# Gated delta rule on one core: the keys of the state scaled on ScalarE, the triangle multiplied in two passes, and TensorE's work put in another order

## The chip, the core and the metric

One core of a Trainium2 chip runs one launch of the whole program. The metric is the device time of that launch in microseconds (us), median of three runs. The engines are TensorE (PE in the rows, its weight loads PEld), VectorE (DVE), ScalarE (ACT), GpSimd (POOL) and SyncE (SP), which issues the DMAs.

## The reference, cut to what matters

The program is four stages on 8 sequences of 512 rows of 256 numbers: attention, a gated FFN with FP4 weights, the gated delta rule, and an FFN with ternary weights. Only the third is touched. Of it:

```
q = l2norm(q) * dk ** -0.5;  k = l2norm(k)            # per head, dk = dv = 128, 8 heads
g = cumsum(g) within chunks of 64 rows
decay = tril(exp(g[i] - g[j]))
tri = tril((k_beta @ k.T) * decay, -1)                # 64 x 64 in each chunk
Tm = inverse(eye + tri)
v_new = Tm @ v_beta;  k_cum = Tm @ (k_beta * exp(g))
for each chunk:                                       # 8 chunks of a sequence, in order
    attn = tril(q @ k.T * decay)
    v_n = v_new - k_cum @ S
    out = (q * exp(g)) @ S + attn @ v_n
    S = S * exp(g_last) + (k * exp(g_last - g)).T @ v_n
```

## The kernel before, in words

**Tiling and staging.** `delta_rule` works on pairs of heads: 8 sequences x 4 pairs are 32 pairs, `e` is the head within a pair. All matmuls are float32; each is issued as two passes, so `x4` in a row of the trace is two matmuls. The loop `for q in range(-1, PAIRS)` runs the scan of pair `q` beside the front of pair `f = q + 1`, and every engine has its own copy of that loop, in program order; semaphores alone tie them together. An iteration has three parts. In the first, `n` goes from 0 to 8: the scan of pair `q` does chunk `m = n`, and the functions `front_early`, `front_middle` and `front_late` lay pieces of the front of pair `f` between its steps (projections `keys_in`, `gate_in`, `values_in`, `queries_in`; the convolution as taps on VectorE; transposes `keys_across`; the products `key_gram`; the norms `key_norms`). In the second, `l` goes from 1 to 5: the levels of the block inverse of pair `f`. At each level TensorE multiplies `NT` by `L` (L2025, "z"), ScalarE copies that to `ZS` (L1516), TensorE multiplies by `U` (L2042 and L2047, "y"), and VectorE puts the result into `U` and `L` (L1605, L1607). The third part makes the attention rows, the new values and the cumulated keys (L2068, L2076).

**A step of the scan.** TensorE multiplies `PQ` by the state `S` (L1981, "p1"); VectorE makes the new values `V2` from it (L1757, "w"), ScalarE copies the query half to `O` (L1503); TensorE multiplies `V2` by the keys `KK` (L1999, "ds"), and VectorE updates `S` (L1773). In odd chunks TensorE multiplies `AT` (L2012, "oi"), and VectorE updates `O` (L1785). The first chunk has no state: its ds takes 64 rows of `VV` and `KK` in place of the 128 rows of `V2` and `KK` that the others take, of which one half is zero.

**What the change touches.** `keys_to_state` (L1561) scales the transposed keys in the PSUM bank `F0` into `KK`, `keys_to_inverse` (L1565) into `KE`, both on VectorE; `values_in` then overwrites `F0`. `lower` (L1592) makes the triangle `NT` = `F1` x `cneg` x `gb`, four instructions for each head, where `cneg` are the norm factors that `key_scales` makes on GpSimd (it ends at L1346) out of the sums of `key_norms` (L1569, L1571), and `gb` the decays. `lower_across` (L1911) transposes `NT`, `first_level` (L1599, L1601) fills `U` and `L` and frees `F1` for `queries_in`. After the last pair of a sequence come the output projection and the residual; in the next pair `statistics` (L1640, L1643) and `normalize` (L1648) run on VectorE at steps 4 and 8.

## Time and profile before

| | us |
|---|---|
| median of 3 runs (lowest, highest) | 3079.18 (3071.64, 3082.57) |
| the profiled execution, its own time | 3079.22 |
| its span | 3077.5 |
| PE busy | 2880.1 (94%) |
| DVE busy | 2246.7 (73%) |
| ACT busy | 1231.3 (40%) |
| POOL busy | 1018.6 (33%) |
| the loop over pairs with scan and front, 1061 to 2806: length | 1745.00 |
| PE, DVE, ACT, POOL busy in it | 1715.55, 1354.44, 742.80, 443.46 |

A row of the timeline has the start, the busy time (of xcount instructions in one run), the engine, the line of the kernel, the operation, the tiles written and read, and in brackets the idle time before it and what ended it. Matmuls are pipelined, and their busy times overlap. How long a run holds TensorE is therefore the distance from its start to the start of the next row, not its busy time.

### The profile page before, as it was taken

What the parts mean: (1) busy time and instruction counts of PE and PEld (TensorE: products, weight loads), DVE (VectorE), ACT (ScalarE), POOL (GpSimd) and SP (SyncE); (2) the same over time, 40 slices, a digit from 0 to 9 for tenths busy, and PEclk for the clock granted to TensorE, in tenths of its full rate; (3) what the DMA queues carried; (4) which work ended last, traced back from release to release, by engine and by line L of the source; (5) the groups of instructions that cost most, each with busy time, mean ns of one, the idle gap of its engine ahead of it and who ended that gap; (6) DMA issues with size and microseconds to landing.
All of it is one profiled execution on the core that took longest, in us unless ns stands there. A gap on an engine that the chain in (4) does not pass through costs nothing. (4 is left out here: it accounts for less than half of the span.)

```text
span 3077.5 us, 81016 instructions
## 1 busy us (share of the span) xinstructions
PE 2880.1 (94%) x32507; PEld 2008.8 (65%) x32507; DVE 2246.7 (73%) x5235; ACT 1231.3 (40%) x2975; POOL 1018.6 (33%) x1495
## 2 busy tenths in 40 slices
PE   6999999849997899999999999999999999998897
PEld 3444444336664677777787777777777777776565
DVE  4666677778885687687788778678678678685566
ACT  1433333413333344344444345345344344342454
POOL 2554555526883222223223222222122222231011
PEclk8999999969998899999999999999999999999899
DMA  2121111100001111010010010100100001000000
GB/s 86 34 52 40 30 31 30 28 7 1 1 1 30 31 47 36 19 33 23 19 36 20 23 33 19 33 23 19 33 23 29 23 23 33 19 19 2 9 21 28
DMA packets 85332, 80.36 MB, mean 26 GB/s; under 512 B 54480, under 2 KB 67808, under 8 KB 84960
## 3 DMA queue, kind: packets, MB, share of 16 engines
q1 hardware_dynamic: 84960, 75.18, 8.7%
q8 instruction: 260, 4.26, 0.6%
q14 instruction: 112, 0.92, 0.1%
HBM read 57.70 MB, written 4.85 MB: 20 GB/s over the span
## 5 line engine op out<-in xcount | busy, mean ns | idle before, releaser
L1842 PE MATMUL gd_bk<-gd_xT,gd_wh 128*128 128x512 f32 x768 | 394.3, 623 | 1.8 <-DVE gd_xT L1742 0.9
L480 DVE TENSOR_REDUCE at_nm<-at_ring 128x2 f32<-128x256 f32 (+3 forms) x256 | 199.1, 820 | 143.1 <-PE at_ring L623 143.1
L1547 DVE SCALAR_TENSOR_TENSOR gd_YK<-gd_bk,gd_cw,gd_YK 128x511 f32<-128x511 f32 (+2 forms) x384 | 283.1, 743 | 10.3 <-ACT gd_YK L1413 4.7
L1516 ACT COPY gd_ZS<-gd_bk 128x256 f32<-128x256 f32 x320 | 119.1, 372 | 299.0 <-PE gd_bk L2025 292.7
L2025 PE MATMUL gd_bk<-gd_L,gd_NT 64*64 64x64 f32 x5120 | 203.3, 222 | 14.4 <-DVE gd_L L1607 7.3
L1605 DVE COPY_PREDICATED gd_U<-gd_mU,gd_bk 128x128 f32<-128x128 int32 x320 | 103.8, 326 | 146.7 <-PE gd_bk L2047 112.2
L2025 PEld LDWEIGHTS gd_bk<-gd_L,gd_NT 64*64 64x64 f32 x5120 | 170.1, 134 | 61.3 <-issue 33.6
L2042 PE MATMUL gd_bk<-gd_U,gd_ZS 64*64 64x64 f32 x5120 | 207.6, 221 | 0.1
L2042 PEld LDWEIGHTS gd_bk<-gd_U,gd_ZS 64*64 64x64 f32 x5120 | 174.7, 135 | 40.9 <-issue 37.1
L302 POOL TENSOR_TENSOR at_PT<-at_PT,at_dm 128x1024 f32<-128x1024 f32 (+3 forms) x128 | 197.8, 1545 | 10.7
L561 PE MATMUL at_ring<-at_QT,at_KT 32*128 32x512 f32 (+3 forms) x1024 | 168.6, 504 | 17.5 <-DVE at_PT L452 12.7
L1842 PEld LDWEIGHTS gd_bk<-gd_xT,gd_wh 128*128 128x128 f32 x768 | 127.5, 192 | 86.2 <-issue 72.1
L1503 ACT COPY gd_O<-gd_bk 64x128 f32<-64x128 f32 x448 | 105.7, 259 | 194.1 <-PE gd_bk L1981 191.9
L1999 PEld LDWEIGHTS gd_bk<-gd_V,gd_KK 128*128 128x128 f32 x896 | 125.4, 190 | 74.1 <-DVE gd_V L1757 54.0
L1999 PE MATMUL gd_bk<-gd_V,gd_KK 128*128 128x128 f32 x896 | 151.3, 291 | 15.7 <-DVE gd_V L1757 13.3
L1981 PEld LDWEIGHTS gd_bk<-gd_S,gd_PQ 128*128 128x128 f32 x896 | 129.9, 192 | 52.3 <-issue 39.1
L1757 DVE SCALAR_TENSOR_TENSOR gd_V<-gd_bk,gd_cneg,gd_VV 64x128 f32<-64x128 f32 x448 | 138.3, 347 | 33.5 <-PE gd_bk L1981 30.1
L1323 POOL TENSOR_TENSOR gd_zz<-gd_zz,gd_nw_row 128x512 f32<-128x512 f32 x64 | 80.2, 1274 | 248.1 <-ACT gd_zz L1435 248.1
L2047 PE MATMUL gd_bk<-gd_ZS,gd_U 64*64 64x64 f32 x4096 | 162.0, 218 | 0.0
L336 ACT ACTIVATE at_PT<-at_ring 128x1024 f32<-128x1024 f32 (+3 forms) x128 | 90.1, 704 | 178.8 <-PE at_ring L561 178.8
L299 POOL TENSOR_SCALAR_AFFINE_SELECT at_PT<-at_PT 128x256 f32<-128x256 f32 x128 | 54.1, 423 | 296.0 <-ACT at_PT L336 295.3
L338 ACT ACTIVATE at_PT<-at_PT 128x1024 f32<-128x1024 f32 (+3 forms) x128 | 94.3, 737 | 138.9 <-DVE at_PT L452 138.7
(355 smaller groups left out, 6755.5 us busy)
## 6 DMA issues: line engine op xcount, KB each, us to landing
...
gd_gb<-gates SPq DMA_DIRECT2D x128, 64.0 KB, 3.3
...
at_QT<-at_QS SPq DMA_DIRECT2D x128, 32.0 KB, 2.0
at_KT<-at_KS SPq DMA_DIRECT2D x128, 32.0 KB, 2.0
at_OC<-at_Ob SPq DMA_DIRECT2D x128, 32.0 KB, 2.0
at_RC<-inverse SPq DMA_DIRECT2D x128, 32.0 KB, 1.8
...
```

The source lines that it names most:

```text
L302: nc.gpsimd.tensor_tensor(PT[s % RP][:, 2:GH, 0:n], PT[s % RP][:, 2:GH, 0:n], dm[:, 0:n].unsqueeze(1).broadcast_to([P, 2, n]), ALU.mult).t ...
L480: nc.vector.tensor_reduce(nm[v % 2][:, k, c0:c0 + HS + 1:HS], set_of(s, 2 + p)[:, :, 0:n], AX.X, ALU.max).then_inc(max_done, 1)
L561: last_ = nc.tensor.matmul(set_of(s, p)[:, i, 0:n], KT[lane(u)][r, k * P:(k + 1) * P], QT[lane(u)][r, k * P:W], start=True, stop=True)
L1516: nc.scalar.copy(ZS[e][:, :, :], chunks(A_[e])).then_inc(zs_done[e], 1)
L1547: nc.vector.scalar_tensor_tensor(out[:, s:W], bank_[:, 0:W - s], cw[:, j, head(f, e), CONVK - 1 - s:CONVK - s], out[:, s:W], ALU.mult, ALU ...
L1757: nc.vector.scalar_tensor_tensor(V2[e][rows(c), t % 2, c, :], A_[e][rows(c), 0:DK], cneg[q % 2][rows(c), e, t:t + 1], VV[e][rows(c), t, :] ...
L1842: ins = nc.tensor.matmul(out[:, :], wh[:, k, e, col * DK:(col + 1) * DK], xT[:, k, :], start=k == 0, stop=k == DC - 1)
L1981: nc.tensor.matmul(A_[e][:, 0:DK], PQ[e][q % 2][:, m // CPT, m % CPT, :, :].rearrange("p s n -> p (s n)"), S[e][:, :], start=True, stop=Tr ...
L1999: nc.tensor.matmul(A_[e][:, DK:2 * DK], fixed, moving, start=True, stop=True).then_inc(ds_mm[e], 1)
L2025: last = nc.tensor.matmul(A_[e][rows(c), t * CK:(t + 1) * CK], NTm[e][rows(c), t, :], L[e][rows(c), t, :], start=True, stop=True)
L2042: last = nc.tensor.matmul(A_[e][rows(c), (TPS + t) * CK:(TPS + t + 1) * CK], ZS[e][rows(c), t, :], U[e][rows(c), t, :], start=True, stop=True)
L2047: last = nc.tensor.matmul(A_[e][rows(c), t * CK:(t + 1) * CK], U[e][rows(c), t, :], ZS[e][rows(c), t, :], start=True, stop=True)
```

## The change

It does this, all in the delta rule:

- `keys_to_state` goes from VectorE (one 128x512 instruction a head) to ScalarE (four 128x128), at n = 3 and 4; `keys_to_inverse` comes on VectorE to n = 3 and 4, both `key_norms` to the end of n = 4.
- `lower` becomes one VectorE instruction a head (`F1` x `gb`), without the wait for the norm factors; GpSimd multiplies `NT` by `cneg` behind `key_scales`.
- The first chunk's ds takes 128 rows like the others; ScalarE copies 64 rows of `VV` into `V2` for it.
- On TensorE both `lower_across` stand together at n = 7, all `queries_in` at n = 8, both `values_across` together at level 3, and the last `values_in` of head 1 is cut into two halves around the ds of step 6.
- Taps are spread otherwise over the levels, `queries_out(f, 0)` goes from level 3 to 5 on ScalarE, `statistics` to the start of a pair, `normalize` to the first step of the pair after.

```diff
@@ gpsimd, key_scales
                     nc.gpsimd.tensor_scalar(cneg[f % 2][:, :, :], cc[:, :, :], -1.0, 0.0, ALU.mult, ALU.add).then_inc(rk_done, 1)
+                    pool.wait_ge(rk_done, f + 1)
+                    for e in E2:
+                        pool.wait_ge(ng_done, f * 2 + e + 1)
+                        nc.gpsimd.tensor_tensor(NTm[e][:, :, :], NTm[e][:, :, :], cols(cneg[f % 2][:, e, :])[:, :, 0:CK], ALU.mult).then_inc(nt_done[e], 1)
@@ scalar
+                def keys_to_state(f, e):
+                    act.wait_ge(kk_done[e], f + 1)
+                    for t in range(TPS):
+                        last = nc.scalar.activation(KK[e][f % 2][:, t, :], F0[e][:, t * P:(t + 1) * P], ACT.Copy, scale=column(KF_, f, e, t))
+                    last.then_inc(ks_done[e], 1)
...
                         gate_out(f, 1)
+                        keys_to_state(f, 0)
+                    if n == 4:
+                        keys_to_state(f, 1)
...
-                        if l == 3 and has(f):
-                            queries_out(f, 0)
                         if l == 4 and has(q):
                             heads_out(q, 0)
                             heads_out(q, 1)
                         if l == 5 and has(f):
+                            queries_out(f, 0)
                             queries_out(f, 1)
...
                             for c in range(CPT):
-                                last = nc.scalar.copy(PQ[e][f % 2][:, :, c, c, :], chunks((A_[e], F1[e])[c]))
-                            last.then_inc(kc_done[e], 1)
+                                nc.scalar.copy(PQ[e][f % 2][:, :, c, c, :], chunks((A_[e], F1[e])[c]))
+                        for e in E2:
+                            act.wait_ge(vnc_done[e], f + 1)
+                            nc.scalar.copy(V2[e][rows(0), 0, 0, :], VV[e][rows(0), 0, :]).then_inc(kc_done[e], 1)
@@ vector, lower
-                    dve.wait_ge(rk_done, f + 1)
                     dve.wait_ge(e_done[e], f + 1)
                     dve.wait_ge(gk_mm[e], f + 1)
                     ge(dve, z_mm[e], f * (LEVELS - 1))
-                    for t in range(TPS):
-                        last = nc.vector.scalar_tensor_tensor(NTm[e][:, t, :], F1[e][:, t * CK:(t + 1) * CK], cneg[f % 2][:, e, t:t + 1],
-                                                              gb[e][f % 2][:, t, :], ALU.mult, ALU.mult)
-                    last.then_inc(nt_done[e], 1)
+                    nc.vector.tensor_tensor(NTm[e][:, :, :], chunks(F1[e]), gb[e][f % 2][:, :, :], ALU.mult).then_inc(ng_done, 1)
@@ vector, the loop
+                        if n == 0 and ends_seq(q - 1):
+                            statistics(seq(q - 1))
...
-                        if n == 4 and ends_seq(q - 1):
-                            statistics(seq(q - 1))
-                        if n == 8 and ends_seq(q - 1):
-                            normalize(seq(q - 1))
+                        if n == 0 and ends_seq(q - 2):
+                            normalize(seq(q - 2))
@@ tensor
                 def values_in(f, e, k):
-                    pe.wait_ge(kk_done[e], f + 1)
+                    pe.wait_ge(ks_done[e], f + 1)
                     project(F0[e], e, 2, k, vp_mm[e])
+
+                def values_half(f, e, half):
+
+                    cut = slice(half * W // 2, (half + 1) * W // 2)
+                    ins = nc.tensor.matmul(F0[e][:, cut], wh[:, DC - 1, e, 2 * DK:3 * DK], xT[:, DC - 1, cut], start=False, stop=half == 1)
+                    if half == 1:
+                        ins.then_inc(vp_mm[e], 1)
...
                                 if m == 0:
-                                    pe.wait_ge(vnc_done[e], q + 1)
                                     pe.wait_ge(kc_done[e], q + 1)
-                                    fixed, moving = KK[e][q % 2][rows(c), t, :], VV[e][rows(c), t, :]
```

Three places of the program as the engines get it, each within one ordinary pair. First TensorE at the start of a pair, before and then of the change (L1842 and L1845 are `keys_in`, L1999 and L2007 ds, L1981 and L1994 p1):

```order
L2076 MATMUL gd_bk<-gd_U,gd_KE 128x64 x16
L1842 MATMUL gd_bk<-gd_xT,gd_wh 128x512 x2
L1999 MATMUL gd_bk<-gd_VV,gd_KK 128x128 x2
L1842 MATMUL gd_bk<-gd_xT,gd_wh 128x512 x2
L1981 MATMUL gd_bk<-gd_S,gd_PQ 128x128 x2
```

```order
L2080 MATMUL gd_bk<-gd_U,gd_KE 128x64 x16
L1845 MATMUL gd_bk<-gd_xT,gd_wh 128x512 x2
L2007 MATMUL gd_bk<-gd_V,gd_KK 128x128 x2
L1845 MATMUL gd_bk<-gd_xT,gd_wh 128x512 x2
L1994 MATMUL gd_bk<-gd_S,gd_PQ 128x128 x2
```

The order is the same; the ds between the two projections now reads `V2`, 128 rows of it. Second, TensorE from p1 of step 6 to the second level, before and of the change (L1911 and L1920 are `lower_across`, L2012 and L2019 oi, L2025 and L2032 z, L1878 the halves):

```order
L1981 MATMUL gd_bk<-gd_S,gd_PQ 128x128 x2
L1842 MATMUL gd_bk<-gd_xT,gd_wh 128x512
L1999 MATMUL gd_bk<-gd_V,gd_KK 128x128 x2
L1911 MATMUL gd_bk<-gd_identc,gd_NT 64x64 x8
L1981 MATMUL gd_bk<-gd_S,gd_PQ 128x128 x2
L1911 MATMUL gd_bk<-gd_identc,gd_NT 64x64 x8
L1999 MATMUL gd_bk<-gd_V,gd_KK 128x128 x2
L2012 MATMUL gd_bk<-gd_V,gd_AT 64x128 x4
L1842 MATMUL gd_bk<-gd_xT,gd_wh 128x512 x2
L2025 MATMUL gd_bk<-gd_L,gd_NT 64x64 x16
L1842 MATMUL gd_bk<-gd_xT,gd_wh 128x512 x2
L2042 MATMUL gd_bk<-gd_U,gd_ZS 64x64 x8
```

```order
L1994 MATMUL gd_bk<-gd_S,gd_PQ 128x128 x2
L1878 MATMUL gd_bk<-gd_xT,gd_wh 128x256
L2007 MATMUL gd_bk<-gd_V,gd_KK 128x128 x2
L1878 MATMUL gd_bk<-gd_xT,gd_wh 128x256
L1994 MATMUL gd_bk<-gd_S,gd_PQ 128x128 x2
L1920 MATMUL gd_bk<-gd_identc,gd_NT 64x64 x16
L2007 MATMUL gd_bk<-gd_V,gd_KK 128x128 x2
L2019 MATMUL gd_bk<-gd_V,gd_AT 64x128 x4
L1845 MATMUL gd_bk<-gd_xT,gd_wh 128x512 x4
L2032 MATMUL gd_bk<-gd_L,gd_NT 64x64 x16
L2048 MATMUL gd_bk<-gd_U,gd_ZS 64x64 x8
```

The first transpose of `NT` has moved behind p1 of step 7, next to the second, and the second head's query projection from behind z of level 1 to ahead of it. Third, VectorE from the update of `S` of step 4 into step 5, before and of the change (L1757 and L1760 are w, L1773 and L1776 the update of `S`, L1571 and L1582 the sums of the norms, L1592 and L1601 `lower`):

```order
L1773 SCALAR_TENSOR_TENSOR gd_S<-gd_S,gd_egl_row,gd_bk 128x128 x2
L1569 TENSOR_TENSOR gd_DG<-gd_bk,gd_identc 128x256
L1571 TENSOR_REDUCE gd_ssk<-gd_DG 128x4
L1561 TENSOR_TENSOR gd_KK<-gd_bk,gd_tab 128x512
L1757 SCALAR_TENSOR_TENSOR gd_V<-gd_bk,gd_cneg,gd_VV 64x128 x2
L1565 TENSOR_TENSOR gd_KE<-gd_bk,gd_tab 128x512
L1773 SCALAR_TENSOR_TENSOR gd_S<-gd_S,gd_egl_row,gd_bk 128x128 x2
L1785 SCALAR_TENSOR_TENSOR gd_O<-gd_O,gd_tab,gd_bk 128x128 x2
L1592 SCALAR_TENSOR_TENSOR gd_NT<-gd_bk,gd_cneg,gd_gb 128x64 x4
```

```order
L1776 SCALAR_TENSOR_TENSOR gd_S<-gd_S,gd_egl_row,gd_bk 128x128 x2
L1580 TENSOR_TENSOR gd_DG<-gd_bk,gd_identc 128x256
L1582 TENSOR_REDUCE gd_ssk<-gd_DG 128x4
L1580 TENSOR_TENSOR gd_DG<-gd_bk,gd_identc 128x256
L1582 TENSOR_REDUCE gd_ssk<-gd_DG 128x4
L1760 SCALAR_TENSOR_TENSOR gd_V<-gd_bk,gd_cneg,gd_VV 64x128 x2
L1601 TENSOR_TENSOR gd_NT<-gd_bk,gd_gb 128x256
L1776 SCALAR_TENSOR_TENSOR gd_S<-gd_S,gd_egl_row,gd_bk 128x128 x2
```

`KK` has gone, `KE` of the second head stands ahead of this piece now, where the first head's norm stood; both norms are together ahead of w of step 5, and a head's triangle is one instruction.

## Rows read from the trace of the kernel before

**Rows 1.** Busy time of each engine, the loop over pairs.
```profile
1061.00:2806.00 1745.00, 1715.55 (x25199) 1346.19 (x25198) 1354.44 (x3635) 742.80 (x2024) 443.46 (x874) 1.00 0.08 26
```

**Rows 2.** Timeline of TensorE, the start of an ordinary pair.
```profile
1789.87 1.98 PE L1842 MATMUL gd_bk<-gd_xT,gd_wh 128*128 128x512 f32 x4
1791.78 0.71 PE L1999 MATMUL gd_bk<-gd_VV,gd_KK 64*128 64x128 f32 x4
1792.42 1.98 PE L1842 MATMUL gd_bk<-gd_xT,gd_wh 128*128 128x512 f32 x4
1794.24 0.61 PE L1981 MATMUL gd_bk<-gd_S,gd_PQ 128*128 128x128 f32 x4
```

**Rows 3.** Timeline of TensorE, a ds between matmuls of its own shape.
```profile
1799.03 0.61 PE L1999 MATMUL gd_bk<-gd_V,gd_KK 128*128 128x128 f32 x4
1799.48 0.60 PE L1876 MATMUL gd_bk<-ident,gd_kT 128*128 128x128 f32 x4
```

**Rows 4.** Timeline of TensorE, steps 6 and 7 of the same pair.
```profile
1809.91 0.61 PE L1981 MATMUL gd_bk<-gd_S,gd_PQ 128*128 128x128 f32 x4
...
1811.22 0.61 PE L1999 MATMUL gd_bk<-gd_V,gd_KK 128*128 128x128 f32 x4
1811.75 0.68 PE L1911 MATMUL gd_bk<-gd_identc,gd_NT 64*64 64x64 f32 x16
1812.37 0.71 PE L1981 MATMUL gd_bk<-gd_S,gd_PQ 128*128 128x128 f32 x4
...
1814.26 0.65 PE L2012 MATMUL gd_bk<-gd_V,gd_AT 64*64 64x128 f32 x8
```

**Rows 5.** Timeline of TensorE, step 8 and level 1.
```profile
1814.85 1.98 PE L1842 MATMUL gd_bk<-gd_xT,gd_wh 128*128 128x512 f32 x4
1816.76 1.15 PE L2025 MATMUL gd_bk<-gd_L,gd_NT 64*64 64x64 f32 x32
1817.84 1.98 PE L1842 MATMUL gd_bk<-gd_xT,gd_wh 128*128 128x512 f32 x4
...
1821.73 0.68 PE L2025 MATMUL gd_bk<-gd_L,gd_NT 64*64 64x64 f32 x16
```

**Rows 6.** Timeline of ScalarE, the copy behind the last of these rows.
```profile
1822.46 0.37 ACT L1516 COPY gd_ZS<-gd_bk 128x256 f32<-128x256 f32 x1 [1.40 <-PE gd_bk L2025]
```

**Rows 7.** Timeline of VectorE, end of step 4 and step 5.
```profile
1806.57 0.68 DVE L1561 TENSOR_TENSOR gd_KK<-gd_bk,gd_tab 128x512 f32<-128x512 f32 x1
1807.27 0.63 DVE L1757 SCALAR_TENSOR_TENSOR gd_V<-gd_bk,gd_cneg,gd_VV 64x128 f32<-64x128 f32 x2
...
1809.82 0.86 DVE L1592 SCALAR_TENSOR_TENSOR gd_NT<-gd_bk,gd_cneg,gd_gb 128x64 f32<-128x64 f32 x4 [0.17 <-POOL gd_cneg L1346]
```

**Rows 8.** Timeline of GpSimd in the same pair.
```profile
1793.18 1.20 POOL L1310 TENSOR_TENSOR gd_gb<-gd_gb,gd_tab 128x256 f32<-128x256 f32 x2
...
1809.58 0.20 POOL L1346 TENSOR_SCALAR gd_cneg<-gd_cc 128x8 f32<-128x8 f32 x1
```

**Rows 9.** Timeline of ScalarE at the start of the ordinary pair, last copies of `PQ`.
```profile
1789.99 0.65 ACT L1536 COPY gd_PQ<-gd_bk 128x256 f32<-128x256 f32 x2 [0.25 <-PE gd_bk L2076]
```

**Rows 10.** Windows: an ordinary pair; the seven pairs after a sequence's end, summed.
```profile
1791.78:1843.90 52.12, 51.64 (x798) 40.36 (x797) 44.02 (x114) 23.89 (x65) 13.45 (x27) 1.00 0.09 27
...
sum 382.30, PE 367.45 PEld 285.25 DVE 319.47 ACT 167.79 POOL 107.63; mean PE 52.49 PEld 40.75 DVE 45.64 ACT 23.97 POOL 15.38
```

**Rows 11.** Timeline of VectorE in one of the seven, 1735.41 to 1789.87.
```profile
1737.85 0.52 DVE L1767 COPY gd_S<-gd_bk 128x128 f32<-128x128 f32 x2 [2.24 <-PE gd_bk L1999]
...
1752.71 1.39 DVE L1640 BATCH_NORM_STATS2 gd_stats<-gd_y 128x6 f32<-128x256 f32 x4
1754.02 0.36 DVE L1643 BATCH_NORM_AGGREGATE gd_mv<-gd_stats 128x2 f32<-128x6 f32 x4
...
1764.69 1.38 DVE L1648 TENSOR_SCALAR X<-gd_y,gd_mv,gd_rstd 128x256 f32<-128x256 f32 x4
```

**Rows 12.** Timeline of VectorE, w of step 1 of the ordinary pair.
```profile
1794.67 0.63 DVE L1757 SCALAR_TENSOR_TENSOR gd_V<-gd_bk,gd_cneg,gd_VV 64x128 f32<-64x128 f32 x2 [0.40 <-PE gd_bk L1981]
```

More of the change, by code:

```diff
@@ L1705, in front_early @@
                     if n == 3:
-                        keys_to_state(f, 0)
+                        keys_to_inverse(f, 0)
                     if n == 4:
-                        key_norms(f, 0)
+                        keys_to_inverse(f, 1)
                     if n == 5:
-                        keys_to_inverse(f, 1)
-                    if n == 6:
-                        lower(f, 1)
+                        lower(f, 0)
                     if n == 7:
@@ L1744, in _ @@
                     for c in range(CPT):
-                        last = nc.vector.memset(V2[e][rows(1 - c), :, c, :], 0.0)
-                last.then_inc(v2_clear, 1)
+                        nc.vector.memset(V2[e][rows(1 - c), :, c, :], 0.0)
                 for q in range(-1, PAIRS):
@@ L1862, in gate_in, with queries_in @@
                         last.then_inc(zp_mm[i], 1)
-                def queries_in(f, e):
+                def queries_in(f, e, k):
                     pe.wait_ge(u_done[e], f * LEVELS + 1)
-                    for k in range(DC):
-                        project(F1[e], e, 0, k, qp_mm[e])
+                    project(F1[e], e, 0, k, qp_mm[e])
                 def values_in(f, e, k):
-                    pe.wait_ge(kk_done[e], f + 1)
+                    pe.wait_ge(ks_done[e], f + 1)
                     project(F0[e], e, 2, k, vp_mm[e])
+                def values_half(f, e, half):
[3 more added lines that the diff above has]
+                        ins.then_inc(vp_mm[e], 1)
                 def keys_across(f, e):
@@ L1947, in front_early @@
                     if n == 6:
-                        values_in(f, 1, 1)
+                        values_half(f, 1, 0)
                     if n == 7:
+                        lower_across(f, 0)
                         lower_across(f, 1)
-                    if n == 8:
-                        queries_in(f, 0)
                 def front_late(f, n):
@@ L1969, in front_late @@
                     if n == 6:
-                        lower_across(f, 0)
+                        values_half(f, 1, 1)
+                    if n == 8:
+                        queries_in(f, 0, 0)
+                        queries_in(f, 0, 1)
+                        queries_in(f, 1, 0)
+                        queries_in(f, 1, 1)
                 x_in(0, 0)
@@ L1995, in _ @@
                                     pe.wait_ge(o1_done[e], q * RS + m)
[L1996 to L1999 removed]
+                                nc.tensor.matmul(A_[e][:, DK:2 * DK], KK[e][q % 2][:, t, :], V2[e][:, t % 2, c, :], start=True, stop=True).then_inc(ds_mm[e], 1)
                         for e in E2:
@@ L2010, in _ @@
                                 for c in range(CPT):
-                                    moving = VV[e][rows(c), t, :] if t == 0 and c == 0 else V2[e][rows(c), t % 2, c, :]
-                                    last = nc.tensor.matmul(B_[e][rows(c), 0:DK], AT[e][q % 2][rows(c), t, :], moving,
+                                    last = nc.tensor.matmul(B_[e][rows(c), 0:DK], AT[e][q % 2][rows(c), t, :], V2[e][rows(c), t % 2, c, :],
                                                             start=True, stop=True)
@@ L2027, in _ @@
                                 last.then_inc(z_mm[e], 1)
-                        if l == 1 and has(f):
-                            queries_in(f, 1)
                         if l == 3 and has(f):
                             values_across(f, 0)
+                            values_across(f, 1)
                         if l == 4 and has(q):
@@ L2049, in _ @@
                                 last.then_inc(y_mm[e], 1)
-                        if l == 3 and has(f):
-                            values_across(f, 1)
                         if l == 5 and ends_seq(q):
```

32 lines of the change are left out of this document (13 added, 19 removed).

## The prediction

> **What bounds the kernel now.** I read the busy times of the engines by stretch first. In the loop over pairs, which the change is about, TensorE is busy 1715.55 of 1745.00 us, and no other engine comes near that [rows 1]. The reader is to see that whatever leaves VectorE there (1354.44 us) is worth nothing by itself: time comes only out of what TensorE does, or out of the places where TensorE waits. So I read next the timeline of TensorE through one ordinary pair, by the distance from one start to the next. Two things stand out.
>
> The first is what a change of tile shape costs. A ds between neighbours of its own shape holds TensorE from 1799.03 to 1799.48, 0.45 us [rows 3]. The ds of the first chunk, which uses 64 rows where its neighbours use 128, holds it from 1791.78 to 1792.42, 0.64 us. The projection ahead of it takes 1.91 us and the one behind it, which is followed by its own shape, 1.82 us [rows 2]. So each side on which a run of 128x128 matmuls meets another shape costs it 0.09 us; a projection with its own shape on both sides would take 1.73 us. The Trainium skill has the same as a rule in "TensorEngine Tiling (Array Packing)", Key Properties: going from one tiling mode to another drains TensorE. It names no price, so the sum goes by the rows.
>
> The second is that the waits of an ordinary pair are short. They are at the levels, where z waits for what VectorE and ScalarE make of the level before, and at ds of step 5, where w starts only when VectorE has got through `KK` [rows 7]. An ordinary pair lasts 52.12 us, of which TensorE shows 51.64 busy. The seven pairs that follow a sequence's end sum to 382.30 us, which is 17.46 us above seven ordinary ones [rows 10]; these are the pairs that carry `statistics` and `normalize` on VectorE [rows 11].
>
> **The change part by part.** The sum is made against the profiled execution's own 3079.22 us, which is the median (3079.18) for all purposes. A pair has 31 instances with scan and front together.
>
> *The ds of the first chunk with 128 rows.* From the first projection to p1 it takes 4.37 us now [rows 2]. With one shape, the first projection keeps the seam at its start (1.82), ds takes 0.45, the second projection 1.73: 4.00 us, a gain of 0.37. Its price is two ScalarE copies of 64x128 ahead of `kc_done`, each at most the 0.37 us of a 128x256 copy [rows 6]. The two last copies of `PQ` there start at 1789.99 and take 0.65 us [rows 9], and ds is due at 1791.78 [rows 2], so 0.74 us more on ScalarE fits by 0.4 us. If it did not, each 0.1 us late would be 0.1 us of the gain gone.
>
> *`lower_across` together, the projection in halves.* From p1 of step 6 to oi of step 7 it takes 4.35 us now [rows 4]. Taking one 64x64 block out from between ds and p1 frees two sides of 0.09 us, and two blocks in one run cost less than apart: one of x16 takes 0.62 us [rows 4], one of x32 takes 1.08 [rows 5], not 1.24. That is 0.34 us. Against it, ds of step 6 has only half a projection between itself and p1. At step 1, p1 starts at 1794.24 [rows 2], and w of both heads starts at 1794.67 and takes 0.63 us [rows 12]; ds of the second head can thus start some 1.1 us behind p1 or a little later, which is when TensorE would reach it. The update of `S` before p1 of step 7 has a similar margin, a little below nothing. I charge 0.15 us for the two, with bounds of 0 and 0.5 (0.5 if w of step 6 comes as late as it does now behind the triangle). Left: 0.19 us.
>
> *`queries_in` of the second head ahead of level 1.* From 1814.85 to 1821.73 it is 6.88 us [rows 5]: 1.91 for the projection, 1.08 for z, 1.91 for the other projection, and 1.98 for y. After: 1.91 and 1.73 for both projections, z 0.99 (one side less), y 1.93. But the projection also covered the copy to `ZS`. At level 2, where nothing covers it, z starts at 1821.73 [rows 5] and the copy runs from 1822.46 for 0.37 us [rows 6]; y can so start 1.20 us after z at the earliest, where z ends after 0.99. With that 0.21 us the piece takes 6.77 us, a gain of 0.11 (bounds: a loss of 0.1 if ScalarE's copy is queued behind `queries_first`, a gain of 0.35 if the seams alone counted).
>
> *`values_across` together.* It takes two sides of a seam away and also the cover that the second one gave to the last level's update before z of level 4. I put it at 0, between a gain and a loss of 0.3 us, the size of the seams around a block.
>
> *Keys on ScalarE.* Four instructions of 128x128 a head; the nearest row is 0.37 us for 128x256 [rows 6], which bounds it by 1.5 us a head from above; half of that, as for half the columns, from below. I take 1.1. ScalarE is busy 742.80 of 1745.00 us [rows 1], and `values_in` of a head, which needs `F0` free, stands a whole step of the scan behind them. Hidden by the idle 57% of ScalarE; with that cover gone it costs 2.2 us a pair.
>
> *VectorE's load.* `KK` leaves twice (0.68 us each), and eight instructions of `lower` (0.86 us a head [rows 7]) become two of 128x256. But at the one place where TensorE waits for it, ahead of w of step 5, one `KK` of 0.68 us [rows 7] is replaced by the other head's norm, two instructions of half its columns each, and the norm ahead of the update of `S` by one `KE`. w of step 5, which starts at 1807.27 [rows 7], stays there within 0.1 us. The rest of the relief falls where TensorE does not wait: 0, with a bound of 0.3 us a pair gained.
>
> *The triangle's second factor on GpSimd.* The nearest row is `gb` x `G_` of the same size, 1.20 us for two [rows 8]. `cneg` is ready at 1809.78 [rows 8], the products are then there about 1810.5 and 1811.1. TensorE reaches the two `lower_across` at about 1812.2. So 1 us of slack, and no cost. Behind this wait on GpSimd are only the output scales, which wait for step 8 anyway. By the Trainium skill's "SBUF — State Buffer", Who interferes with whom, a VectorE instruction with two SBUF inputs and a GpSimd one that reads SBUF block each other; w, the update of `S` and the taps that run then have one input in PSUM each, so the rule would change nothing here, and no row shows such a block.
>
> *`statistics` and `normalize`.* `statistics` takes 1.39 + 0.36 us, and VectorE is idle 2.24 us at the pair's start, where it goes [rows 11]: free. `normalize` (1.38 us [rows 11]) goes between the taps and w of step 1, ahead of which VectorE idles 0.40 us [rows 12], and w ends at 1795.30, a little ahead of the next ds; I let that be worth 0.4 us. That leaves 0.6 us in each of seven pairs. So 17.46 - 4.2 = 13.3 us are gained, if all that these pairs have above the others comes from the two.
>
> **The sum.** 31 x (0.37 + 0.19 + 0.11) = 20.8 us, and 13.3 us: 34.1 us. 3079.2 - 34.1 = 3045.
>
> **The rivals.**
>
> - *Seams and waits both go* (chance 0.13). What speaks for it is that VectorE is some 2 us a pair lighter and w would come sooner in steps 5 and 6, and that no wait appears at the halves or at level 1. That gives 0.15 + 0.21 + 0.3 us more a pair, 20 us: 3025. Against it: w of step 5 is held by the same amount of work as before.
> - *The new waits eat the seams* (0.17). The copy to `ZS`, the half projection and the lost cover at level 4 all charge their upper bounds, (0.1 + 0.11) + (0.5 - 0.15) + 0.3 us a pair, 27 us: only the 13 us of `normalize` and `statistics` are left, less a part: 3072, hardly to be told from no change.
> - *Slower: the triangle comes late* (0.10). TensorE, in order, stands at `lower_across` at step 7 and with it ds of the step, until GpSimd is through. It decides from about 1.1 us of lateness a pair above the slack: 31 x 1.1 = 34 us. It takes GpSimd products of 1.7 us instead of 0.6 us each, or norms that come 2 us later. At 2.2 us late it would be 3113. What speaks against it is the row of `gb` [rows 8]; what speaks for it is that the norms, both now behind the update of `S`, leave the chain norm, factors, product, transpose no slack but that 1 us.
> - *The forecast* (0.60).
>
> **How the numbers follow.** The forecast's own range is 3032 to 3060, by the bounds of its terms. The whole range goes up to the second rival and a little over it and down to the first: 3020 to 3074. About 0.3% (9 us) is what a measurement of this kernel can tell from no change. Faster by more than that: forecast, first rival and a part of the second, 0.77; within it 0.13; slower 0.10.
>
> **What would show it.** The ds of the first chunk holds TensorE 0.45 us and is followed by a projection of 1.73. An ordinary pair lasts 51.4 us, not 52.12. y of level 1 starts 1.2 us behind z. The seven pairs last 52 us, and the next ones 0.6 us more than ordinary ones. `lower_across` shows no idle time ended by GpSimd. Wrong would be it if ordinary pairs had not become shorter, if TensorE's waits for GpSimd's `NT` or for VectorE's w at steps 5 and 6 had grown, or if the seven pairs kept their surplus.

## The result, and the profile after

The changed kernel takes 3062.88 us (median of 5 runs, 3059.48 to 3064.87) against 3079.18 us of the kernel before in the same rounds (5 runs, 3071.64 to 3085.69). The ratio is 0.9943, with a 95% interval of 0.9927 to 0.996: the interval leaves out 1, so the kernel is faster, by 16.3 us between the medians where 34.1 were forecast. The time is inside the range, the direction is right, and the size is about half.

The windows of the launch show where it is to be looked for: first the loop over pairs, then the last scan with its projection, then the stage behind it. First the kernel before, cut at its own borders:

```profile
1058.44:2801.20 1742.76, 1713.96 (x25183) 1344.51 (x25181) 1351.37 (x3625) 742.20 (x2018) 445.45 (x879) 1.00 0.09 26
2801.20:2841.30 40.10, 32.52 (x166) 25.17 (x164) 14.96 (x48) 7.81 (x34) 2.64 (x7) 0.87 0.00 1
2841.30:3077.50 236.20, 199.49 (x977) 137.16 (x977) 147.59 (x300) 110.01 (x214) 26.88 (x52) 0.94 0.06 19
```

The same windows of the changed kernel:

```profile
1059.00:2779.00 1720.00, 1682.62 (x25244) 1349.43 (x25242) 1291.69 (x3377) 823.33 (x2328) 482.30 (x941) 1.00 0.09 26
2779.00:2823.20 44.20, 37.03 (x166) 28.52 (x164) 15.74 (x48) 8.27 (x36) 2.70 (x7) 0.77 0.00 1
2823.20:3061.70 238.50, 201.33 (x978) 138.22 (x977) 147.62 (x300) 110.10 (x214) 26.91 (x52) 0.91 0.06 19
```

From the start of the first pair to the start of the last scan, the loop takes 1742.74 us before and 1721.02 after: 21.7 us less. What lies behind it took 5.4 us more in this execution (the windows above are cut a little ahead of the last scan), with a lower granted clock in both windows (0.87 and 0.77, 0.94 and 0.91). The last of them is code that the change does not touch, so this part is looked at apart from the loop, below.

The timeline of TensorE at the start of an ordinary pair of the changed kernel (L2007 is ds, L1845 a projection, L1994 p1), which answers to [rows 2]:

```profile
1833.12 1.98 PE L1845 MATMUL gd_bk<-gd_xT,gd_wh 128*128 128x512 f32 x4
1834.94 0.61 PE L2007 MATMUL gd_bk<-gd_V,gd_KK 128*128 128x128 f32 x4
1835.39 1.88 PE L1845 MATMUL gd_bk<-gd_xT,gd_wh 128*128 128x512 f32 x4
1837.11 0.61 PE L1994 MATMUL gd_bk<-gd_S,gd_PQ 128*128 128x128 f32 x4
```

From start to start: 1.82, 0.45, 1.72, together 3.99 us where 4.37 stood. That is the forecast 4.00. The same timeline further on, steps 6 and 7 (L1878 the halves, L1920 both `lower_across`, L2019 oi), which answers to [rows 4]:

```profile
1852.95 0.61 PE L1994 MATMUL gd_bk<-gd_S,gd_PQ 128*128 128x128 f32 x4
1853.39 0.60 PE L1878 MATMUL gd_bk<-gd_xT,gd_wh 128*128 128x256 f32 x2
1853.82 0.69 PE L2007 MATMUL gd_bk<-gd_V,gd_KK 128*128 128x128 f32 x4
1854.35 0.60 PE L1878 MATMUL gd_bk<-gd_xT,gd_wh 128*128 128x256 f32 x2
1854.78 0.66 PE L1994 MATMUL gd_bk<-gd_S,gd_PQ 128*128 128x128 f32 x4
1855.37 1.15 PE L1920 MATMUL gd_bk<-gd_identc,gd_NT 64*64 64x64 f32 x32
1856.45 0.71 PE L2007 MATMUL gd_bk<-gd_V,gd_KK 128*128 128x128 f32 x4
1857.09 0.65 PE L2019 MATMUL gd_bk<-gd_V,gd_AT 64*64 64x128 f32 x8
```

p1 to oi takes 4.14 us, before 4.35. Level 1 (L2032 is z, L2048 y), which answers to [rows 5]; y starts 1.15 us behind z:

```profile
1138.80 1.15 PE L2032 MATMUL gd_bk<-gd_L,gd_NT 64*64 64x64 f32 x32
1139.95 0.68 PE L2048 MATMUL gd_bk<-gd_U,gd_ZS 64*64 64x64 f32 x16
```

One place got longer: the projection ahead of ds of step 5. Before, in the pair of [rows 4], it holds TensorE for 1.13 us, and the chain names no wait there:

```profile
1806.55 1.02 PE L1842 MATMUL gd_bk<-gd_xT,gd_wh 128*128 128x512 f32 x2
1807.68 0.76 PE L1999 MATMUL gd_bk<-gd_V,gd_KK 128*128 128x128 f32 x4
```

After, it is 1.30 us, and ds waits for VectorE's w (L1760). This is one of the prediction's own signs of being wrong:

```profile
1849.41 1.02 PE L1845 MATMUL gd_bk<-gd_xT,gd_wh 128*128 128x512 f32 x2
1850.71 0.76 PE L2007 MATMUL gd_bk<-gd_V,gd_KK 128*128 128x128 f32 x4 [0.28 <-DVE gd_V L1760]
```

VectorE's timeline of the changed kernel at this place, which answers to [rows 7], tells why: L1580 and L1582 are the norms of both heads, and w comes behind them.

```profile
1848.61 0.42 DVE L1580 TENSOR_TENSOR gd_DG<-gd_bk,gd_identc 128x256 f32<-128x256 f32 x1
1849.06 0.42 DVE L1582 TENSOR_REDUCE gd_ssk<-gd_DG 128x4 f32<-128x256 f32 x1
1849.40 0.41 DVE L1580 TENSOR_TENSOR gd_DG<-gd_bk,gd_identc 128x256 f32<-128x256 f32 x1
1849.85 0.42 DVE L1582 TENSOR_REDUCE gd_ssk<-gd_DG 128x4 f32<-128x256 f32 x1
1850.30 0.63 DVE L1760 SCALAR_TENSOR_TENSOR gd_V<-gd_bk,gd_cneg,gd_VV 64x128 f32<-64x128 f32 x2
```

The second norm takes 0.90 us until w starts; the `KK` that stood there took 0.70 from its start to w's [rows 7].

The sum of the seven pairs that carry `statistics`, which answers to [rows 10], and then the first and the sum of the seven that now carry `normalize`:

```profile
sum 363.44, PE 355.74 PEld 284.48 DVE 297.36 ACT 185.72 POOL 115.93; mean PE 50.82 PEld 40.64 DVE 42.48 ACT 26.53 POOL 16.56
```

```profile
1333.26:1385.71 52.45, 50.96 (x800) 40.61 (x798) 42.33 (x110) 26.56 (x75) 15.35 (x31) 1.00 0.09 27
...
sum 369.96, PE 357.48 PEld 284.57 DVE 293.44 ACT 185.77 POOL 106.97; mean PE 51.07 PEld 40.65 DVE 41.92 ACT 26.54 POOL 15.28
```

An ordinary pair lasts 51.61 us now. Above seven of them (361.27), the first seven have 2.2 us (before 17.46) and the second seven 8.7 us. Two pairs of the first seven (52.64 and 52.63 us) and three of the second hold a stop of TensorE that is looked at with e8; the other five of the first last 51.60 to 51.72 us and the other four of the second 52.45 to 52.52.

### The profile page after: what moved, and what is told of

It reads as the page before. It is cut to its first block and busy times, and to the rows that moved or that the text cites. A ratio compares the mean times of both kernels' runs of the same rounds, so it can differ in the third digit from the quotient of the medians.

```text
span 3061.7 us, 81240 instructions
## 1 busy us (share of the span) xinstructions
PE 2855.1 (93%) x32571; PEld 2019.8 (66%) x32571; DVE 2186.0 (71%) x4979; ACT 1315.0 (43%) x3295; POOL 1057.2 (35%) x1559
## 5 line engine op out<-in xcount | busy, mean ns | idle before, releaser
L1845 PE MATMUL gd_bk<-gd_xT,gd_wh 128*128 128x512 f32 x704 | 346.6, 612 | 1.1 <-DVE gd_xT L1744 0.9
L2032 PE MATMUL gd_bk<-gd_L,gd_NT 64*64 64x64 f32 x5120 | 207.3, 222 | 20.4 <-DVE gd_L L1614 8.6
L2032 PEld LDWEIGHTS gd_bk<-gd_L,gd_NT 64*64 64x64 f32 x5120 | 172.8, 135 | 63.3 <-DVE gd_L L1614 36.2
L2048 PE MATMUL gd_bk<-gd_U,gd_ZS 64*64 64x64 f32 x5120 | 208.1, 221 | 3.0 <-issue 2.8
L2007 PEld LDWEIGHTS gd_bk<-gd_V,gd_KK 128*128 128x128 f32 x1024 | 144.6, 191 | 79.0 <-DVE gd_V L1760 49.0
L2048 PEld LDWEIGHTS gd_bk<-gd_U,gd_ZS 64*64 64x64 f32 x5120 | 175.0, 135 | 24.1 <-issue 16.0
L2007 PE MATMUL gd_bk<-gd_V,gd_KK 128*128 128x128 f32 x1024 | 175.5, 294 | 14.1 <-DVE gd_V L1760 13.1
L1845 PEld LDWEIGHTS gd_bk<-gd_xT,gd_wh 128*128 128x128 f32 x704 | 120.2, 192 | 94.5 <-issue 91.9
L1760 DVE SCALAR_TENSOR_TENSOR gd_V<-gd_bk,gd_cneg,gd_VV 64x128 f32<-64x128 f32 x448 | 138.7, 348 | 57.3 <-PE gd_bk L1994 50.3
L1994 PEld LDWEIGHTS gd_bk<-gd_S,gd_PQ 128*128 128x128 f32 x896 | 131.1, 192 | 53.6 <-issue 37.9
L1548 ACT COPY gd_PQ<-gd_bk 128x256 f32<-128x256 f32 x128 | 41.4, 375 | 257.5 <-PE gd_bk L2080 257.5
```

The lines of the kernel that those rows point to most:

```text
L1760: nc.vector.scalar_tensor_tensor(V2[e][rows(c), t % 2, c, :], A_[e][rows(c), 0:DK], cneg[q % 2][rows(c), e, t:t + 1], VV[e][rows(c), t, :] ...
L1845: ins = nc.tensor.matmul(out[:, :], wh[:, k, e, col * DK:(col + 1) * DK], xT[:, k, :], start=k == 0, stop=k == DC - 1)
L1994: nc.tensor.matmul(A_[e][:, 0:DK], PQ[e][q % 2][:, m // CPT, m % CPT, :, :].rearrange("p s n -> p (s n)"), S[e][:, :], start=True, stop=Tr ...
L2007: nc.tensor.matmul(A_[e][:, DK:2 * DK], KK[e][q % 2][:, t, :], V2[e][:, t % 2, c, :], start=True, stop=True).then_inc(ds_mm[e], 1)
L2032: last = nc.tensor.matmul(A_[e][rows(c), t * CK:(t + 1) * CK], NTm[e][rows(c), t, :], L[e][rows(c), t, :], start=True, stop=True)
L2048: last = nc.tensor.matmul(A_[e][rows(c), (TPS + t) * CK:(TPS + t + 1) * CK], ZS[e][rows(c), t, :], U[e][rows(c), t, :], start=True, stop=True)
```

## The experiments

Every one of them leaves all arithmetic as it is and differs from the changed kernel by the edit shown, which is shortened. All but the last were run once, profiled. Beside the first eight the kernel before took 3078.5 and 3078.7 us, beside the last three 3073.0 to 3085.2 (7 runs, median 3077.2). "Pair" is the length of an ordinary pair, "loop" from the first pair's start to the start of the last scan, "rest" from there to the last matmul of that scan's projection, and then the last stage (both by their instructions, so not cut quite as the windows above). "Stops" are the places in the loop where TensorE is idle for 0.29 us or more with no semaphore that ends it ("issue" in the trace), and their sum. The reader should compare by pair and loop: the rest varies by more than most effects.

| | total us | pair | loop | rest | stops |
|---|---|---|---|---|---|
| before | 3079.22 | 52.12 | 1742.7 | 39.7, 230.4 | 4, 2.8 |
| changed | 3063.47 | 51.61 | 1721.0 | 42.8, 232.7 | 8, 5.8 |
| e1_ds64 | 3063.5 | 52.01 | 1728.9 | 41.9, 230.5 | 8, 4.5 |
| e2_across_apart | 3059.48 | 51.81 | 1723.2 | 38.6, 233.6 | 4, 2.1 |
| e3_queries_level1 | 3061.46 | 51.73 | 1721.0 | 43.9, 232.1 | 5, 2.6 |
| e4_triangle_dve | 3105.05 | 52.90 | 1760.8 | 40.4, 234.2 | 8, 5.7 |
| e5_keys_dve | 3065.7 | 51.61 | 1721.2 | 43.9, 234.5 | 8, 5.9 |
| e6_norms_apart | 3047.97 | 51.44 | 1716.0 | 38.7, 232.2 | 10, 6.4 |
| e7_normalize_level1 | 3056.22 | 51.62 | 1714.6 | 42.8, 234.6 | 8, 5.5 |
| e8_load_level4 | 3057.41 | 51.61 | 1717.0 | 40.5, 230.6 | 2, 2.3 |
| e9_decays_late | 3051.41 | 51.28 | 1710.7 | 42.8, 230.8 | 8, 5.7 |
| e10_decays_alone | 3059.51 | 51.61 | 1721.0 | 39.6, 234.6 | 7, 5.6 |
| best3 | 3041.1 (median) | 51.28 | 1703.6 | 39.9, 230.2 | 2, 2.5 |

**The first ds with 64 rows again.**

```
-  fixed, moving = KK[e][q % 2][:, t, :], V2[e][:, t % 2, c, :]
+  if m == 0: fixed, moving = KK[e][q % 2][rows(c), t, :], VV[e][rows(c), t, :]
-  nc.scalar.copy(V2[e][rows(0), 0, 0, :], VV[e][rows(0), 0, :]).then_inc(kc_done[e], 1)
```

> The changed kernel with one part undone: the first chunk's ds takes 64 rows of VV and KK again, and ScalarE makes no copy into V2. Seam theory (each meeting of two tile shapes on TensorE costs about 0.09 us a side): an ordinary pair goes from 51.61 us back to 52.0 (+0.39), the projection ahead of ds to 1.91 us, ds to 0.64, the one behind to 1.82; some 12 us over 31 pairs. Rival theory (the gain of the change came from VectorE's lighter load): the pair stays at 51.6. For the tail, the scan of the last pair, which stands alone: if its first wait is the copies into V2 and this pause is what takes the clock down, the wait ahead of the first ds falls from 0.93 to about 0.44 us, the granted clock of the last scan goes up again to the 0.87 of the kernel before and the stretch from the last pair's end to the end of the projection is about 40 us instead of 44; if the clock falls by chance, it stays near 44. Total near 3069.

(The first chunk's oi reads `VV` again too.) The pair grew by 0.40 us, where the rows of the seam give 0.37, so the seam of the 64-row ds is the whole of it within 0.03 us, and the two copies on ScalarE cost the pair nothing. In the last scan the wait ahead of ds is back at 0.44 us, and the stretch takes 41.9 us with a granted clock of 0.80, between the 40 that stood for the pause as cause of the low clock and the 44 that stood for chance. Other runs decide more: e2 and e10 keep the copies and the wait of 0.93 us and have 38.6 and 39.6 us, so the pause alone does not bring the low clock.

**`lower_across` apart, the projection whole.**

```
-  values_half(f, 1, 0) ... lower_across(f, 0); lower_across(f, 1) ... values_half(f, 1, 1)
+  values_in(f, 1, 1)   ... lower_across(f, 1)                     ... lower_across(f, 0)
```

> The changed kernel with one part undone: lower_across of head 0 stands at step 6 again and the last values projection is whole. Seam theory: p1 of step 6 to oi of step 7 goes from 4.15 us back to 4.35, an ordinary pair from 51.61 to 51.8, the total up by 6 us to 3069. If the halves had cost more than the 0.15 us that was charged for them, this kernel would be less than 0.2 us a pair slower. Rival (VectorE's relief): no change.

0.20 us a pair, as the working had it (0.19). Over 31 pairs that is 6 us; the loop is only 2.2 us longer, since TensorE stops four times in it for 2.1 us in place of eight times for 5.8. Its total is below the changed kernel's: that difference lies ahead of the loop and behind it.

**`queries_in` of head 1 back in level 1.**

```
-  queries_in(f, 1, 0); queries_in(f, 1, 1)      # step 8
+  if l == 1 and has(f): queries_in(f, 1, 0); queries_in(f, 1, 1)
```

> The changed kernel with one part undone: the query projection of head 1 stands behind z of level 1 again. Seam theory with the exposed copy to ZS: oi of step 7 to z of level 2 goes from 6.76 + 0.58 back to 6.90 + 0.58 us, an ordinary pair from 51.61 to 51.75, total up by 4 us. If the seams alone counted it would be 0.35 a pair, 11 us. The weights' load, which waits for both query projections, also starts about 1.2 us later; if the idle of TensorE in the middle of a group at level 2 (7 places of 0.5 to 1.2 us, ended by nothing that the profile shows) comes from this load, those places move to z of level 2 and 3, as before the change, or go.

0.12 us a pair (31 x 0.12 = 3.7 us), forecast as 0.11. The loop is nevertheless no longer than the changed kernel's, since TensorE stops five times in it for 2.6 us in place of eight times for 5.8. What these stops hang on is looked at with e8.

**The triangle's two factors in one product on VectorE.**

```
-  nc.vector.tensor_tensor(NTm[e], chunks(F1[e]), gb[e][f % 2], ALU.mult)            # head 1 at step 5
-  nc.gpsimd.tensor_tensor(NTm[e], NTm[e], cols(cneg[f % 2][:, e, :])[:, :, 0:CK], ALU.mult)
+  nc.vector.scalar_tensor_tensor(NTm[e][:, t, :], F1.., cneg.., gb.., ALU.mult, ALU.mult)   # x4, steps 5 and 6
```

> The changed kernel with one part undone: the triangle is made in one product of four instructions a head on VectorE, which wait for the norm factors, at the places of the kernel before; GpSimd makes no product. Theory: TensorE does not care who makes the triangle, but w of step 6 comes late behind it, and the half projection no longer covers that: ds of step 6 waits 0.25 to 0.3 us, an ordinary pair is 51.9. Rival 1: GpSimd's product is just as late as the triangle was, then the pair stays at 51.61 or gets shorter. Rival 2 (VectorE's load counts everywhere): the 1.0 us more of VectorE shows in full, 52.6.

The pair grew by 1.29 us, four times what was expected, and by more than the second rival's 1.0. Timeline of VectorE in this kernel (L1599 is the product, L1760 w of step 6), and of TensorE beside it:

```profile
1187.92 0.86 DVE L1599 SCALAR_TENSOR_TENSOR gd_NT<-gd_bk,gd_cneg,gd_gb 128x64 f32<-128x64 f32 x4 [1.05 <-POOL gd_cneg L1346]
1188.70 0.59 DVE L1760 SCALAR_TENSOR_TENSOR gd_V<-gd_bk,gd_cneg,gd_VV 64x128 f32<-64x128 f32 x2
```

```profile
1187.77 0.60 PE L1878 MATMUL gd_bk<-gd_xT,gd_wh 128*128 128x256 f32 x2
1189.08 0.75 PE L2007 MATMUL gd_bk<-gd_V,gd_KK 128*128 128x128 f32 x4 [0.71 <-DVE gd_V L1760]
```

VectorE stands for 1.05 us at the product, waiting for factors that GpSimd makes of both norms, and w stands behind it. The half projection ahead of ds of step 6 takes 1.31 us instead of 0.43, which is 0.88 of the 1.29; most of the rest is in the second half and p1 behind it (0.26 and 0.09). So the second factor on GpSimd is not worth the few instructions that it takes from VectorE; it takes away a wait in which w was queued. With both norms at step 4, the change depends on it: 40 us.

**Keys on VectorE again.**

```
-  nc.scalar.activation(KK[e][..], F0[e][..], ACT.Copy, scale=column(KF_, f, e, t))    # steps 3, 4
+  nc.vector.tensor_tensor(KK[e][f % 2], tiles(F0[e]), spread(KF_, f, e), ALU.mult)     # steps 3, 5
```

> The changed kernel with one part undone: KK is scaled on VectorE again (128x512 once a head), for head 0 at the end of step 3 and for head 1 at step 5 behind w. Theory: at both places VectorE has time, so an ordinary pair stays within 0.1 us of 51.61 and ScalarE's share was of no use in itself. Rival (VectorE's relief is what pays): 0.6 us or more a pair longer, 52.2, most of it as a wait of ds of step 4 or 6 for w.

Nothing, to 0.01 us a pair: VectorE's lighter load is worth nothing where TensorE does not wait for it.

**The norms a step apart**, head 0's ahead of w of step 5 and head 1's behind it, the first factors of the triangle with them.

```
-  if n == 4: key_norms(f, 0); key_norms(f, 1)
-  if n == 5: lower(f, 1)            # head 0's is earlier in step 5
+  if n == 4: key_norms(f, 0)
+  if n == 5: key_norms(f, 1), behind it lower(f, 0)
+  if n == 6: lower(f, 1)
```

> The changed kernel with one thing more: key_norms of head 1 goes from the end of step 4 behind w of step 5, and the triangle's two products one place later each. Theory: TensorE stands 0.44 us ahead of ds of step 5 in the changed kernel (1.30 us for a projection of 0.86) because w waits behind two norms; with one norm there the projection takes 0.86 to 0.95 us and an ordinary pair 51.2 (-0.40). The factors come 0.7 us later on GpSimd, inside the 1 us of slack. Rival: that slack is not there, lower_across or first_level waits, and the pair stays at 51.6 or gets longer.

Only 0.17 us a pair. The wait at step 5 was the norms': the projection there fell from 1.30 to 0.86 us and its ds from 0.69 to 0.54. But most of it came back one step on. TensorE in this kernel:

```profile
1124.23 0.60 PE L1879 MATMUL gd_bk<-gd_xT,gd_wh 128*128 128x256 f32 x2
1125.06 0.68 PE L2008 MATMUL gd_bk<-gd_V,gd_KK 128*128 128x128 f32 x4 [0.23 <-ACT gd_O L1516]
```

and ScalarE, where the copies of `O` (L1516), for which ds waits, stand behind the exponentials of the next pair's decays:

```profile
1122.61 1.28 ACT L1466 ACT_TABLE_LOAD   x1
1123.90 0.72 ACT L1466 ACTIVATE gd_gb<-gd_gb 128x256 f32<-128x256 f32 x2
1124.65 0.43 ACT L1516 COPY gd_O<-gd_bk 64x128 f32<-64x128 f32 x2
```

**The decays at the pair's end**, alone and together with the norms apart. ScalarE is idle 4.68 us there.

```
-  if n == 5: values_first(f, 0); decays(f + 1, 0); decays(f + 1, 1)     # and the reload of Silu at step 6
+  if l == 5: queries_out(f, 1); decays(f + 1, 0); decays(f + 1, 1); activation(warm, .., ACT.Silu)
```

> Only the decays and the reload moved, both norms of a pair still together at step 4 as in the changed kernel. Theory (the path through steps 5 and 6 goes over VectorE's two norms, and ScalarE's exponentials lie beside them): the ordinary pair stays at 51.6 us within 0.1, the projection ahead of ds of step 5 at 1.30. Rival (ScalarE's exponentials held the changed kernel back too): the pair falls by 0.2 us or more.

> The norms of the two heads at steps 4 and 5 again, and with them the two decay exponentials and the table reload behind them, moved on ScalarE from steps 5 and 6 to the end of the pair, where it stands idle 4.68 us ahead of the last copies and they need 1.28 + 0.72 + 1.28 + 0.20 = 3.5 us. Theory (the half projection ahead of ds of step 6 took 0.82 us in e6 because ScalarE's copies of that step stand behind the table load and the exponentials): it falls back to about 0.43, the ordinary pair from 51.44 to about 51.05, the loop from 1716.0 to about 1704 us. Rival (it is VectorE's product of the triangle at step 6 that holds its step back): 0.82 and 51.44 stay. A second rival: 3.5 us do not fit in the idle time, the last copies of the pair come late, and the pair grows by up to 0.5 us at its end.

Alone they are worth nothing (51.61 us). With the norms apart, 0.16 us a pair and not 0.39. TensorE in that kernel, e9_decays_late:

```profile
1130.13 0.60 PE L1878 MATMUL gd_bk<-gd_xT,gd_wh 128*128 128x256 f32 x2
1130.56 0.69 PE L2007 MATMUL gd_bk<-gd_V,gd_KK 128*128 128x128 f32 x4
...
1131.52 0.66 PE L1994 MATMUL gd_bk<-gd_S,gd_PQ 128*128 128x128 f32 x4
1132.26 1.25 PE L1920 MATMUL gd_bk<-gd_identc,gd_NT 64*64 64x64 f32 x32
```

The half projection is back at 0.43 us, so ScalarE's exponentials were the cause of e6's 0.83. But p1 to `lower_across` is 0.74 us (0.59 in the changed kernel) and `lower_across` to the next ds 1.18 (1.08): the triangle now comes late from GpSimd, which starts it only here, at the norms' new time:

```profile
1131.59 1.18 POOL L1350 TENSOR_TENSOR gd_NT<-gd_NT,gd_cneg 128x256 f32<-128x256 f32 x2
```

So three results are due within a few tenths of a microsecond at steps 5 to 7: w behind the norms, the copies of `O` behind the exponentials, the triangle behind the norms and the factors. Who moves one finds the next.

**`normalize` in level 1 instead of step 1.**

```
-  if n == 0 and ends_seq(q - 2): normalize(seq(q - 2))
+  if l == 1 and ends_seq(q - 1): normalize(seq(q - 1))
```

> The changed kernel with normalize in the same pair as statistics, behind the taps of level 1, where VectorE idles 1.9 us. Theory: the 0.77 us or more that the projection of step 1 takes longer in seven pairs (a pair of 52.46 instead of 51.61) is normalize alone: those pairs go to 51.6 and nothing else moves, 6 us in all. Rival: what these pairs lose comes from the residual or the row scales of GpSimd; then it stays or goes to level 1 of the pair before.

The four pairs that had 52.45 to 52.52 us have 51.61, the three with a stop fell by 0.6 to 0.9, and the loop is 6.4 us shorter. The place in the changed kernel, VectorE (L1655 is `normalize`; w of step 1, L1760, starts behind it at 1786.31) and TensorE:

```profile
1784.79 1.49 DVE L1655 TENSOR_SCALAR X<-gd_y,gd_mv,gd_rstd 128x256 f32<-128x256 f32 x4
```

```profile
1786.72 0.76 PE L2007 MATMUL gd_bk<-gd_V,gd_KK 128*128 128x128 f32 x4 [0.66 <-DVE gd_V L1760]
```

**The load of the next weights held back to level 4.**

```
   sp.wait_ge(qp_mm[e], f)
+  sp.wait_ge(y_mm[e], (f - 1) * (LEVELS - 1) + 4)
```

> The changed kernel with the load of the next pair's weights (1 MB, 5 us) held back until y of level 4 instead of starting when the query projections are through. Theory: TensorE's stops of 0.5 to 1.2 us in the middle of a group at level 2, 7 of them and 5.8 us in all, are instruction fetches that fall into this load; they go, or turn up at level 4 and 5. The weights are wanted 10 us later still, so nothing else waits. Rival: they do not depend on the load and stay at level 2 in the same pairs.

The changed kernel's TensorE stops eight times in the loop, for 0.35 to 1.09 us and 5.8 us together: seven times in the middle of a group of level 2, once at that level's end. By the length of their pairs, against pairs of the same kind without a stop, the eight cost 7.5 us; the four of the kernel before cost 3.4. One of the stops:

```profile
2485.82 0.28 PE L2053 MATMUL gd_bk<-gd_ZS,gd_U 64*64 64x64 f32 x3
2486.74 0.62 PE L2053 MATMUL gd_bk<-gd_ZS,gd_U 64*64 64x64 f32 x13 [0.64 <-issue]
```

The DMA view of the stretch 2478 to 2490 us shows the next pair's 1 MB of weights, whose wait for `queries_in` now ends earlier, and two packets of one instruction queue:

```profile
q1 hardware_dynamic: 272, 1.05, 25.9%
q8 instruction: 2, 0.03, 1.1%
...
gd_wh<-in_L_attn_W_qkvz SPq DMA_DIRECT2D x1, 1024.0 KB, 5.2
```

Held back, all eight are gone from level 2, and the loop is 4.0 us shorter. But two stops, of 0.90 and 1.39 us, now stand in the group of the new values behind level 5, again just behind the load. The longer one:

```profile
2277.70 0.66 PE L2073 MATMUL gd_bk<-gd_VV,gd_U 64*64 64x128 f32 x8 [1.39 <-issue]
```

So it is shown that the stops go where the load goes, and that they are fewer at the later place. How they come about is not shown. A delayed fetch of instructions would fit, but in the changed kernel a packet of 16 KB of that queue lands within 1.8 us of the load's end in all 30 pairs that have a load, in the 22 without a stop as in the eight with one. And e2, whose load comes as early as the changed kernel's, stops only four times: the place of the load is not all that decides.

**All that helped**: e6, e7, e8 and e9's edits together, and the copies to `V2` of a head behind its own `PQ` copies.

> All that helped at once: norms apart, decays at the end of the pair, the layer norm's last part in level 1 of the pair's chain, the load of the next weights held back to level 4, and the V2 copies of a head beside its own state copies. If the parts add up as the single looks gave them (5 + 12 + 6 + 4 us and under 1), the loop takes about 1694 us and the launch about 3036 us, 3028 to 3044. Rival (the parts share their gains, since a step held by one late result is held by the next when that goes): about 3045.

Median of 4 runs 3041.1 us (3037.55 to 3043.04), inside the expected range and between its middle and the rival; the ratio to the kernel before is 0.9876 with an interval of 0.9858 to 0.9893: 36 us faster than before. Its loop is 9.6 us above the expected 1694. The norms and the decays, which share their gain as shown, account for 6.7 of them (17 expected, 5.0 and 5.3 measured). Most of the rest is in two neighbouring pairs of 54.01 and 54.72 us, 5.1 us above their kind, of which e8's loop, from which the 4 us were taken, has 1.7. The first of them ends with one of the two stops that are left, and behind it the granted clock was 0.50 for 6.8 us:

```profile
2266.64 0.65 PE L2072 MATMUL gd_bk<-gd_VV,gd_U 64*64 64x128 f32 x8 [1.62 <-issue]
...
2268.13:2274.96 6.83, 6.83 (x29) 4.49 (x28) 0.54 (x3) 2.35 (x7) 4.01 (x8) 0.50 0.02 5
```

## Why the prediction was half right

*The first ds* (0.37 us a pair): right; 0.38 in the trace and 0.40 in e1. *`lower_across` and the halves* (0.19): right; 0.21, and 0.20 in e2. *`queries_in`* (0.11): right; 0.12 in e3, 1.15 us from z to y where 1.20 was said. The price of a seam, 0.09 us a side, read from three rows, carried all three. The rule of the Trainium skill, "TensorEngine Tiling (Array Packing)", Key Properties, that a change of tiling mode drains TensorE, agrees with them.

*`values_across`* (0, within 0.3): from z of level 2 to z of level 5 it takes 11.93 us where it took 11.89, so a loss of 0.04, within its bounds. *Keys on ScalarE* (0): right (e5), and its price was right: 1.14 us for a head's four instructions, where 1.1 was said. *The triangle on GpSimd* (0): right, 1.18 us for both, where [rows 8] gave 1.20, and through 0.7 us ahead of `lower_across` where 1 us was said. The slower rival, a late triangle, did not come; e9 shows how near it lay.

*VectorE's load ahead of w of step 5* is the first step that failed: "w of step 5 [...] stays there within 0.1 us". The working let a norm, "two instructions of half its columns each", stand for one `KK`. Columns were halved, but two instructions that depend on each other take 0.90 us from start to w, not 0.70. That is the 0.17 us that TensorE loses there, 5.3 us in 31 pairs. With it the ordinary pair is at -0.51 us and not -0.67 (15.8 us, not 20.8).

*`statistics`* (free): right. *`normalize`* (0.6 us in each of seven): mis-sized. VectorE's idle time and the room behind w were valued at 0.4 us each, but taps and `normalize` together push w so far that ds waits 0.66; each of the seven has 0.85 us (52.46 against 51.61). That is 1.8 us over the forecast 4.2. And the move was for nothing: at step 8 `normalize` had cost no time. An undisturbed one of the seven pairs lasted 53.73 us before, 1.61 above an ordinary one, and the projection ahead of w of step 5, where `statistics` stood, has all of that (2.74 us in place of 1.13). Put in level 1, as in e7, it costs nothing again; left at step 8 of the changed kernel it was not tried.

*The 17.46 us* were taken as the two's own, "if all that these pairs have above the others comes from the two". Only 7 x 1.6 = 11.3 us of it is a direct cost, all of `statistics`: before, TensorE waits 1.7 us in each of the seven for w of step 5. Three pairs last 53.73 us by that alone; a fourth, of 54.46, has a stop of 0.66 us besides. The other three last 55.4 to 55.8. One of them, its wait and a window of the stretch behind it:

```profile
1302.28 0.76 PE L1999 MATMUL gd_bk<-gd_V,gd_KK 128*128 128x128 f32 x4 [1.71 <-DVE gd_V L1757]
...
1303.80:1307.20 3.40, 3.40 (x8) 1.85 (x8) 2.45 (x12) 1.13 (x3) 0.34 (x1) 0.50 0.00 0
```

In these three the granted clock was 0.50 for 3.4 us behind the wait: 1.7 to 2.1 us more a pair, 5.5 us in all. So the 17.46 are 11.3 of `statistics`, 5.5 of the clock and 0.7 of a stop. The changed kernel's loop shows no such stretch of low clock. This gain was in the sum without its being known, and that much of it was luck.

*What was not in the sum*: the stops. Eight in place of four; by their pairs they cost 7.5 us in place of 3.4. Of the 3.4, 0.7 lay in one of the seven pairs and had been counted as gained with the 17.46, so against the forecast the stops take 4.8 us. The step that the prediction passed over is this: `queries_in` moved ahead of level 1 also releases the weight load earlier. The projection that the load waits for ended 2.99 us behind the start of z of level 1 before [rows 5], and ends with it now, so the load ends within level 2. e3 and e8, which move the load later again, have fewer stops; since e2 has too, with the load as early, this is the likely cause of the increase and not a proven one. Every instruction that waits for a moved one should have been followed, SP's too.

So the loop: 34.1 forecast, less 5.0 (ordinary pairs), 1.8 (`normalize`) and 4.8 (stops). Another 1.0 us is the last pair's, which lasts 52.61 us and not 51.6, because the loop as measured here ends with the last scan's first ds, and that waits 0.93 us for the copies to `V2`. That leaves 21.5; 21.7 were measured.

*Behind the loop* the profiled execution lost 5.4 us more, and 0.6 us ahead of it. The wait at the last scan's first ds, just ahead of this border, is the change's own. It was 0.44 us before, for `PQ`, so it costs 0.5 us in one launch:

```profile
2780.02 0.71 PE L2007 MATMUL gd_bk<-gd_V,gd_KK 128*128 128x128 f32 x4 [0.93 <-ACT gd_V L1551]
```

The 5.4 us are not the change's own as far as the runs show: they move from kernel to kernel with the same code there, or nearly the same: the last scan with its projection took 38.6 to 43.9 us over the runs of the table, the last stage 230.2 to 234.6, at different granted clocks. Whether the change makes the low clock in the last scan more likely stays open: the kernel before has one profile, with 39.7, and the others lie on both sides of it. The mean granted clock of the whole launch does point that way: 0.966 to 0.970 in the five runs of the changed kernel, 0.969 to 0.975 in the ten of the kernel before that have one.
